# Both layer norms' last step and the residual sum on GpSimd, the key projection first in step 3, and three weights made ready before the first turn

## The reference

```python
x = emb[ids]                                  # 64 sequences of 128 tokens, 256 features
q, k, v = x @ Wq.T + bq, x @ Wk.T + bk, x @ Wv.T + bv      # 16 heads of 16
attn = softmax(q k^T / sqrt(16))              # per head, 128 x 128
h = (attn v) @ Wo.T + bo
n = layernorm(h)                              # (h - mean) / sqrt(var + 1e-5)
Bu = (n @ B_w.T) @ C_w.T
s[t] = sum over i<t of decay^(..) * Bu[i]     # exclusive scan along the sequence
h = h + sigmoid(n @ gate_w.T + gate_b) * s
out = h + layernorm(h) @ sign(weight).T
```

## Time and profile before

| | |
|---|---|
| time before, median of 3 runs | 780.36 us (780.24 to 781.73) |
| the profiled execution's own time | 785.06 us |
| its span | 782.9 us |
| mean granted clock of TensorE, share of full speed | 0.976 |
| PE busy / PEld busy | 90% / 83% of the span |
| DVE busy / ACT busy / POOL busy | 74% / 74% / 26% of the span |

### The profile page before, as it was taken

One profiled execution on the slowest core, in us unless ns is written; L12 is line 12 of the kernel. 1 busy time (PEld: TensorE's weight loads), 2 busy tenths in 40 slices (PEclk: granted clock), 3 DMA queues, 4 the chain that ended last, 5 costly groups with the idle time before them and its releaser, 6 DMA issues.

```text
span 782.9 us, 21221 instructions
## 1 busy us (share of the span) xinstructions
PE 703.9 (90%) x7047; PEld 650.6 (83%) x7047; DVE 579.0 (74%) x1307; ACT 576.9 (74%) x1643; POOL 205.1 (26%) x271
## 2 busy tenths in 40 slices
PE   1379899999999999999999999999999999999864
PEld 0268889888899899989889899989999899989753
DVE  4345688777777887777777887777787888778663
ACT  2178787787888787788788788788888788788610
POOL 7200132133222332233222332233222332221121
PEclk9889999999999999999999999999999999999985
DMA  5232222333333223333333222333333222332000
GB/s 136 94 95 82 68 78 76 95 109 108 96 107 95 71 78 90 107 107 107 94 107 95 72 80 88 107 107 107 94 107 103 71 75 86 107 108 95 15 14 27
DMA packets 56015, 69.67 MB, mean 89 GB/s; under 512 B 6768, under 2 KB 41648, under 8 KB 55984
## 3 DMA queue, kind: packets, MB, share of 16 engines
q1 hardware_dynamic: 52048, 60.48, 24.2%
q0 software_dynamic: 3072, 8.39, 5.7%
q10 hardware_dynamic: 864, 0.40, 0.2%
HBM read 10.52 MB, written 8.39 MB: 24 GB/s over the span
## 4 chain that ended last, share of the span: by engine, by line
PE 45%; DVE 15%; SPq 11%; DMA 11%; issue 9%; ACT 7%; POOL 1%; DVEq 1%; ACTq 0%; another core or an unknown queue 0%; POOLq 0%
PE ps_g L635 23%; DMA q_stack<-q_low 9%; SPq L237 8%; PE ps_t L707 7%; PE ps_s L635 5%; PE ps_c L635 4%; PE ps_g L684 3%; SPq L242 3%; DVE neg_max L497 3%; ACT k_high L399 3%; DVE xn L530 2%; DVE gated L589 2%; PE ps_g L733 2%; DVE v_aug L578 2%; ACT probs L353 2%
## 5 line engine op out<-in xcount | busy, mean ns | idle before, releaser
L353 ACT ACTIVATE probs<-ps_s,neg_max 128x128 f32<-128x128 f32 x1024 | 298.1, 397 | 99.1 <-DVE neg_max L497 99.1
L497 DVE TENSOR_REDUCE neg_max<-ps_s 128x4 f32<-128x512 f32 x256 | 176.2, 688 | 144.4 <-PE ps_s L635 135.9
L362 ACT COPY probsT<-ps_t 128x512 f32<-128x512 f32 x256 | 156.2, 610 | 31.2 <-PE ps_t L707 29.5
L707 PE MATMUL ps_t<-ident,probs 128*128 128x128 f32 x1024 | 156.0, 275 | 5.3 <-ACT probsT L362 5.1
L635 PE MATMUL ps_s<-k_stack,q_stack 128*128 128x256 f32 x512 | 125.6, 327 | 14.4 <-DMA q_stack<-q_low 13.6
L707 PEld LDWEIGHTS ps_t<-ident,probs 128*128 128x128 f32 x1024 | 119.3, 141 | 14.2 <-issue 4.5
L635 PEld LDWEIGHTS ps_s<-k_stack,q_stack 128*128 128x128 f32 x512 | 78.4, 194 | 20.7 <-DMA q_stack<-q_low 20.0
L292 POOL TENSOR_TENSOR state_high<-state_in,ones_col 128x512 fp32r<-128x512 f32 x32 | 33.2, 1036 | 199.1 <-DVE state_in L624 199.1
L305 POOL TENSOR_TENSOR rs<-ve,neg_half 128x2 f32<-128x2 f32 x32 | 22.1, 692 | 217.9 <-DVE ve L524 217.9
L283 POOL DMA_INDIRECT x_emb<-in_emb,id_col x64 | 64.9, 1014 | 36.3 <-PE ps_g L684 20.4
L635 PE MATMUL ps_c<-probsT,v_aug 128*32 128x128 f32 x2048 | 69.3, 276 | 0.0
(11 more groups left out here) (126 smaller groups left out, 1866.7 us busy)
## 6 DMA issues: line engine op xcount, KB each, us to landing
k_stack<-k_high SPq DMA_DIRECT2D x128, 128.0 KB
q_stack<-q_high SPq DMA_DIRECT2D x64, 256.0 KB
k_stack<-k_low SPq DMA_DIRECT2D x64, 128.0 KB
q_stack<-q_low SPq DMA_DIRECT2D x32, 256.0 KB
out<-y SPq DMA_DIRECT2D x32, 256.0 KB, 2.1
x_emb<-in_emb,id_col POOLq DMA_INDIRECT x64, 4.3
raw<-in_wkT SPq DMA_DIRECT2D x1, 256.0 KB, 3.1
raw<-in_wqT SPq DMA_DIRECT2D x1, 256.0 KB, 4.1
```

The costliest lines, as they stand in the source:

```text
L353: last = nc.scalar.activation(probs[s % 2][:, j], ps_s[s % 2][:, j * SEQ:j * SEQ + SEQ], ACT.Exp, bias=neg_max[s % 2][:, j:j + 1])
L362: nc.scalar.copy(probsT[st][:], ps_t[:]).then_inc(act_pT, 1)
L497: nc.vector.tensor_reduce(neg_max[s % 2][:], ps_s[s % 2][:].rearrange("p (h k) -> p h k", h=HPS), axis=AX.X, op=ALU.max, negate=True).then ...
L707: last = nc.tensor.transpose(ps_t[:, j * SEQ:j * SEQ + SEQ], probs[st % 2][:, j], ident[:])
```

## The change

Four things are changed.

1. `norm_apply` leaves VectorE. GpSimd does it in a new function `normalise`: subtract the mean (128x512, the mean broadcast), then the power as before, then multiply by `rs` (128x512, broadcast). The transposes of `xn1` and `xn2` wait on semaphores of GpSimd.
2. The residual sum `h1` is a GpSimd `tensor_tensor` add of 128x512 in place of the one on VectorE.
3. In step 3 the key projection stands ahead of the second half of the context and of the transposition of `xn1` on TensorE; `k_high` moves ahead of the move of `xn1` on ScalarE; `k_low` moves ahead of the fifth maximum on VectorE, and the second half of the context's normalisation behind the statistics of the second norm.
4. Only the key, query and value weights are made ready ahead of the first turn. The rest of the preparation stands ahead of turn 0, and TensorE waits for it ahead of turn 1. The product that makes the state weight is put in `ps_c` and no longer in `g3`.

```diff
-        def turns(eng, turn):
+        def turns(eng, turn, ahead=()):
             for t in range(-2, 6):
+                for at, prepare in ahead:
+                    if t == at:
+                        prepare()
                 turn(t, t % 2)
...
+            def normalise(pair, prev, h, mv, ve, rs, xn, freed, centred, rs_done, done):
+                await_event(pool, freed, 1, prev, 1)
+                nc.gpsimd.tensor_tensor(xn[:], h[:], mv[:, :, 0:1].to_broadcast([P, 2, D]),
+                                        ALU.subtract).then_inc(centred, 1)
+                nc.gpsimd.tensor_tensor(rs[:], ve[:], neg_half[:], ALU.pow).then_inc(rs_done, 1)
+                await_event(pool, centred, 1, pair, 1)
+                await_event(pool, rs_done, 1, pair, 1)
+                nc.gpsimd.tensor_tensor(xn[:], xn[:], rs[:].unsqueeze(2).to_broadcast([P, 2, D]),
+                                        ALU.mult).then_inc(done, 1)
...
                 if exists(t - 2):
                     await_event(pool, dve_ve1, 1, t - 2, 1)
-                    await_event(pool, dve_xn1, 2, t - 3, 2)
-                    nc.gpsimd.tensor_tensor(rs1[:], ve1[:], neg_half[:], ALU.pow).then_inc(rs1_done, 1)
+                    normalise(t - 2, t - 3, h0[par], mv1, ve1, rs1, xn1, pe_xn1T, centred1, rs1_done, pool_xn1)
                 copy_ids(t + 2, par)
                 if exists(t - 3):
+                    await_event(pool, dve_gated, 1, t - 3, 1)
+                    await_event(pool, dve_y, 1, t - 4, 1)
+                    nc.gpsimd.tensor_tensor(h1[:], gated[:], h0[1 - par][:], ALU.add).then_inc(pool_h1, 1)
+                if exists(t - 3):
                     await_event(pool, dve_ve2, 1, t - 3, 1)
-                    await_event(pool, dve_xn2, 2, t - 4, 2)
-                    nc.gpsimd.tensor_tensor(rs2[:], ve2[:], neg_half[:], ALU.pow).then_inc(rs2_done, 1)
+                    normalise(t - 3, t - 4, h1, mv2, ve2, rs2, xn2, pe_xn2T, centred2, rs2_done, pool_xn2)
                 gather(t + 2, par)
...
-            act.wait_ge(small_loaded, 96)
-            nc.scalar.activation(e_ld[:], ld_col[:], ACT.Exp, scale=-1.0).then_inc(exp_ld, 1)
...
-                if exists(t - 2):
-                    norm_apply(t - 2, h0[par], mv1, rs1, xn1, rs1_done, pe_xn1T, dve_xn1)
                 if exists(t - 3):
                     await_event(dve, pe_sums, 1, t - 3, 1)
                     await_event(dve, act_tanh, 1, t - 3, 1)
...
-                if exists(t - 3):
-                    await_event(dve, dve_gated, 1, t - 3, 1)
-                    await_event(dve, dve_y, 1, t - 4, 1)
-                    nc.vector.tensor_tensor(h1[:], gated[:], h0[1 - par][:], ALU.add).then_inc(dve_h1, 1)
-
-                maxima(3)
+
+                maxima(3)
+                if exists(t - 3):
+                    norm_stats(t - 3, h1, pool_h1, stats2, dve_st2)
+
+                if exists(t - 3):
+                    await_stats(t - 3, dve_st2, pool_xn2)
                 context_norm(1, g2)
-                if exists(t - 3):
-                    norm_stats(t - 3, h1, dve_h1, stats2, dve_st2)
-
-                if exists(t - 3):
-                    await_stats(t - 3, dve_st2, dve_xn2)
+                if exists(t + 1):
+                    split_low(k_low, g1, bk_col, k_high, act_khi, dve_klo)
                 maxima(4)
...
-            turns(dve, turn)
+            turns(dve, turn, ((0, prepare),))
...
             pe.wait_ge(ids_ready, 1)
-            pe.wait_ge(w_low, 6)
-            pe.wait_ge(prep_done, 1)
-            pe.wait_ge(powers_made, 2)
+            pe.wait_ge(w_low, 3)
...
                 attention(3)
+                if exists(t + 1):
+                    await_event(pe, dve_xlo, 1, t + 1, 1)
+                    await_first((dve_ctx, 2, t - 1, 1), (dve_klo, C, t, C))
+                    feature_major(g1, wk, xT, pe_k)
                 if exists(t - 1):
                     await_first((dve_v, 1, t, 1), (dve_h0, 1, t - 2, 1))
                     context_rows(1, g2)
                 if exists(t - 2):
-                    await_event(pe, dve_xn1, 2, t - 2, 2)
+                    await_event(pe, pool_xn1, 1, t - 2, 1)
...
-                if exists(t + 1):
-                    await_event(pe, dve_xlo, 1, t + 1, 1)
-                    await_first((dve_ctx, 2, t - 1, 1), (dve_klo, C, t, C))
-                    feature_major(g1, wk, xT, pe_k)
...
-            turns(pe, turn)
+            turns(pe, turn, ((0, turn_powers), (1, await_prepared)))
```

134 lines of the change are left out of this document (68 added, 66 removed).

## The result

The changed kernel takes 753.31 us, the median of 4 runs (751.42 to 753.67), against 780.48 (780.24 to 781.73) for the kernel before on the same chip: ratio 0.9644, 95% interval 0.9628 to 0.9661. The forecast was 754.0. Run again later, on chip 0, the same kernel took 779.82 against 786.86, ratio 0.9911 [0.9883, 0.9939] (`after_again`). So there are two questions: do the steps of the forecast hold, and where do 26 us go in the later run.

The account below looks back on a forecast made before the run. TensorE, busy 90%, was taken as bound by its own work with the k_low wait, and by the k_high-to-q_low chain through SyncE. −14.4 − 14.0 − 3 + 5.3 = −26.1 gave 759.0, less 4.7 for the median: 754, range 744 to 772.

Parts of the forecast that it names:

- The start: Before the first scores: embeddings turned at 10.9 instead of 25.27, scores at 25.1; −14.4 us, bounds −11 to −15.
- The lock that L463 showed: Start: VectorE instruction stalled to 4.19 us behind GpSimd's zero fill; a repeat on the first small tensor_scalar priced 0 to 1.5.
- The first turns: Turns 0 to 4: longer waits on the q_low DMA shrink as the query's parts come 0.6 to 0.8 earlier; −3 us.
- A full turn: Turns 5 to 30: 0.43 gained at the gate, 0.11 from the DMA; 0.54 each, bounds 0 and 0.9, −14.0 in all.
- The end: Last pairs: GpSimd's norms and h add latency that nothing covers; +5.3 us, bounds 3 and 7.
- The level: Whole kernel: profiled execution 785.06 against median 780.36; the same 4.7 difference taken off 759.0 gives 754.
- Rival 2: Every turn: GpSimd and VectorE lock each other out, up to 2.1 us per turn; 812 us, chance 0.07.
- Rival 1: Full turn gives nothing: h on GpSimd is 0.4 us or more later and holds the gate; 769 us, chance 0.16.
- rival 3: Start: preparation still holds the first turns, 5 to 8 us of 14.4 are lost; 761 us, chance 0.09.
- Both are covered: Full turn: later second norm, and gathers issued 2.5 us later but wanted 10 us on, cost nothing.

Follow-up runs that it names:

- before_again: The kernel before, unaltered, profiled once more in one run: 784.37 us, period 22.00.
- start_only: Kernel before with only the shortened preparation (three weights ahead of the first turn): 773.54 us, ratio 0.9846.
- gather_late: Changed kernel, with GpSimd's gather for pair 2 in turn 0 held until turn 0's first scores: 778.63 us, ratio 0.9891 to the kernel before.
- order_only: Kernel before with only the new order around step 3, norms and the sum h still on VectorE: 792.24 us, ratio 1.0078.
- gpsimd_only: Kernel before with only both norms' last step and the sum h moved to GpSimd, old order and start: 772.22 us, ratio 0.9833.
- tail_on_vector: Changed kernel, with both norms' last step and h on VectorE in the turns past the last pair: 773.98 us, ratio 0.9834 to the kernel before.
- h_on_vector: Changed kernel, with the sum h back on VectorE behind the fourth maximum: 770.06 us, ratio 0.9778 to the kernel before.

## Why the prediction came out right, and where it didn't

The terms, in the two profiles (782.9 to 751.3, −31.6; the forecast for this span was −26.1):

| term | forecast | measured |
|---|---|---|
| first scores | −14.4 | −11.75 (39.49 to 27.74) |
| from there to the expansion of turn 7 | −4.1 | −10.1 (150.41 to 140.33) |
| 23 turns from there | −12.4 | −14.2 (0.62 each) |
| two turns to the expansion of turn 32 | −0.5 | −2.4 (43.27 to 40.84) |
| the end | +5.3 | +6.9 (43.89 to 50.74) |

The forecasts of the second to fourth row are the −3 of the first turns and the 26 turns at 0.54, shared out. Of the −2.4 in the fourth row, 1.5 lie in this profile of before alone: the same two turns take 41.77 in `before_again` and 41.76 in `start_only`.

- **The start** was right in kind and 2.65 short. The embeddings are turned at 11.76, not 10.9, since the gather landed later; and the first scores stand behind a `q_low` transfer that starts at 23.55 and takes 4.2 us to let them go, against 2.5 before, with the gathers of pair 2 beside it (`gather_late`: 2.51). The lock that L463 showed met the next instruction in line, but small: `e_ld` took 0.94 and ended with GpSimd's zero fill (20.04 + 1.83), and the 128x512 instruction that took 4.19 takes 0.55. L463 itself had begun inside an earlier fill, that of `k_stack` (16.21 + 3.54), and ended 0.28 behind the one that followed; the prediction names the second alone.

```profile
20.97 0.94 DVE L480 TENSOR_SCALAR e_ld<-e_ld 128x2 f32<-128x2 f32 x1
24.70 0.55 DVE L495 TENSOR_SCALAR raw<-raw 128x512 f32<-128x512 f32 x1
28.64 1.29 DVE L518 TENSOR_REDUCE neg_max<-ps_s 128x4 f32<-128x512 f32 x2 [1.13 <-PE ps_s L641]
```

  VectorE was 1.13 us early for the first maxima, so the moved preparation cost nothing.
- **The first turns** were the mis-sized term: −10.1 for −4.1. I took them to gain 0.6 each; from first scores to first scores they gain 1.71, 1.07, 1.95, 1.17, 2.11, 1.13 and 0.94 in turns 0 to 6, most of which had waited 0.4 to 1.6 us for the `q_low` DMA before. I took these waits to be shortened by 3 us in all; they are gone. Their place was misread too: not nearly all of the 6.7 us lie in the turns 0 to 4, but 4.3, with 1.0 at the two turns behind and 1.5 spread over the loop. What takes the waits away is the order, by TensorE's waits on this DMA in `order_only` (of 7.8 the first scores' is 6.7: 1.1 left) and `start_only` (14.4, 4.5 of it the first: 9.9 left), where before has 6.7 left; in `gpsimd_only` it is 6.7 again. With `k_high` first on ScalarE, SyncE has the key's issues behind it when the query's parts come: in the turn shown they end at 438.36 and the query's start at 438.98, where before they follow at once (470.12, 470.17). The waits are about half of the −10.1. Over this stretch the parts alone give −2.3 (`order_only`), −3.7 (`gpsimd_only`) and +2.8 (`start_only`), −3.2 in sum; the rest comes only when they are together, and no run had two of them.

```profile
PE ps_s L635 <- DMA q_stack<-q_low: 7.8, 3, 6.7
```
```profile
PE ps_s L642 <- DMA q_stack<-q_low: 14.4, 14, 4.5
```

- **A full turn**: 0.62 for 0.54, but made up otherwise. Forecast: 0.43 at the gate, 0.11 from the DMA. Measured: 0.15 from expansion to context, 0.21 at the gate, 0.25 from gate to expansion. The turn shown in the earlier trace rows had waited 0.55, and others 0.45; the new wait is 0.38 there and 0.21 in the next. The path was as written (`h`, statistics, context, `k_low`, maximum, `xn1Tl`), the durations were 1.04, 1.04 and 1.30, VectorE stood 0.97 for `h` and not 0.8. The chain from `k_high` through SyncE gave more than its 0.11; `order_only` has the same 8.36 in its last stretch, so the order earned it.
- **The end**: +6.9 for +5.3, within its bounds, but made up otherwise. At a granted clock of 0.76 in this stretch before has 43.89 and `after_again`, the same program as after, 48.36: 4.5 longer. The result's profile has 50.74 at 0.67, so some 2.4 us of the 6.9 come with the lower clock, which the sum had no term for. `tail_on_vector` has 43.5 at 0.82: with the norms and `h` back on VectorE the surplus is gone, the clock's part with it. For the last pair `ve` to the end of `xn` is 3.1 us:

```profile
740.40 1.04 POOL L294 TENSOR_TENSOR xn<-h,mv 128x512 f32<-128x512 f32 x1 [1.42 <-DVE ve L545]
741.40 0.70 POOL L296 TENSOR_TENSOR rs<-ve,neg_half 128x2 f32<-128x2 f32 x1
742.25 1.04 POOL L299 TENSOR_TENSOR xn<-xn,rs 128x512 f32<-128x512 f32 x1
```

- **The level.** The profile of before was 4.6 us above its median (785.06 to 780.48), that of after 0.3 below (753.01 to 753.31). Taken span to span the sum was 5.5 short; the shift of 4.7 from the profile's level to the median's hid that. The hit at 754.0 is luck to this extent: two errors of about 5 us against each other. The level goes with the granted clock. Of the eleven runs of before on chip 3 the one at 780.1 has 0.986, the others, 784.59 to 787.42, have 0.975 to 0.978; the profile of before has 0.976, and all four runs of after have 0.971 to 0.978. The clocks of the runs of before beside the result aren't on record, so that its median of 780.48 belongs to the higher level is likely and not shown.
- **The rivals.** Rival 2 (a lock in every turn) is wrong: VectorE's value and embedding parts, at 430.07 and 430.67 beside GpSimd's scaling (430.30 to 431.34), take 0.68 each. Rival 1 is wrong in the result. In `after_again` a turn is even 0.38 longer than before, by a way that the rival didn't name. Of rival 3's 5 to 8 us at the start 2.65 came true.
- **What the prediction missed** is one sentence: the gathers are issued 2.5 us later, "Both are covered". Their landing is covered. What happens beside them isn't: in the changed kernel the gathers stand over `ps_c`'s reports, and ScalarE's queue behind `ctx_raw` (tanh, `xn2Th`, the probabilities) leads to the expansion. The trace of before had shown it once, in turn 0 (2.38 us). In the result's profile it cost nothing; on the three other chips on which turns of the changed kernel with gathers were profiled (10, 0 and 15) it cost 0.9 to 1.0 us in each. Why it stays away in the one is open.
- **What the order is worth then.** Where the increments come late, parts 1 and 2 in the old order have a period of 21.49 (`gpsimd_only`, chip 3), and the whole change has 22.37 (`gather_late`, `after_again`). By these rows the new order gives 0.1 us a turn in the result and loses 0.9 elsewhere. Parts 1, 2 and 4 in the old order were not run; an estimate, `gpsimd_only` less the 12.8 us of `start_only`, is 759 us or 0.97 of before, where the whole change has 0.99. It compares different chips, and the parts don't simply add.

## What to carry to other kernels

- Moving work to an idle engine and reordering for it must be tried together and apart: the order alone made this kernel 0.8% slower, the move alone gave 0.51 us of a turn, both gave 0.62 in the result and lost 0.38 elsewhere. Move what nobody waits for (the norm's last step) and keep what stands on the path (the sum `h`: 0.2 us a turn lost, `h_on_vector`); and in the turns without cover at the end put it back (6 to 7 us, part of it by a higher granted clock).
- Look up every wait of the first trace that has no named releaser, even if it comes once: the 2.38 us in turn 0 came back as 2 us in every turn when the order changed.
- Look at what is reported while GpSimd issues an indirect DMA, and repeat a result on another chip before you believe a few per cent: the same instructions gave 3.6% and 0.9%.
- Give the granted clock beside every stretch that you compare: the same program's end took 50.7 us at 0.67 and 48.4 at 0.76.

## What was not expected of the hardware

- Increments of TensorE on a semaphore that fell due while GpSimd issued its two gathers were recorded 1.3 to 1.8 us late in `gather_late` and 1.0 to 1.3 in `gpsimd_only`, against the even spacing of 0.22 us that they have otherwise. In both the last of them comes 3.0 us behind the first gather's start and 1.6 behind the second's (medians of 18 turns). In the latter the turn is still 21.49. In the result's trace, with the gathers at the same place as in `gather_late`, none is late.
- A GpSimd instruction of 128x512 with one operand broadcast takes 1.04 us (mean of 128), with two full ones 1.28 to 1.30. The Trainium skill, page "GPSIMD Engine Reference", section 3.1, puts two-input elementwise work at about 2.6 cycles per element against VectorE's one, and doesn't tell a broadcast operand from a full one. In time the rows are 1.5 and 1.9 times VectorE's 0.68 to 0.69; the measured numbers decide.
- From the issue of the `q_low` transfer to the scores that wait for it were 2.5 us, and 4.2 with two gathers beside it. Whether the gathers slowed the transfer or the report of its end is not told apart.
